# A GpSimd power over an unread 128x2 tile behind each of 512 transfers by index

## The chip, the core and the metric

The kernel runs on one core of a Trainium2 chip. A core has TensorE (PE in the profile, its weight loads PEld), VectorE (DVE), ScalarE (ACT), GpSimd (POOL) and SyncE (SP), each with an instruction stream of its own, run in the order written; they meet only at semaphores. Sixteen DMA engines move data for all of them. A DMA whose rows are picked by a table of indices is issued from GpSimd here, a DMA with transposition from SyncE. The metric is the time of one execution on the device in microseconds, the median of several.

## What is computed

A small transformer of two layers over x, 32 x 256 tokens of width 128, each step a residual:

```python
x = x + 0.5 * _L0_ffn_ref(_layernorm(x), ...)   # 8 experts, the best 2 of each token, and a shared one
x = x + _L0_attn_ref(_layernorm(x), ...)        # attention without softmax, group norm, projection
x = x + 0.5 * _L0_ffn_ref(_layernorm(x), ...)   # the same expert layer again
x = x + 0.5 * _L1_ffn_ref(x, ...)               # 8 experts, the best 1, gelu
x = x + _L1_attn_ref(x, ...)                    # gated linear attention, a scan over time
x = x + 0.5 * _L1_ffn_ref(x, ...)
```

The expert layer of the first kind is what the change touches. For each token it multiplies with the weights of two experts only:

```python
idx = jax.lax.top_k(biased, TOP_K)[1]
cw = jnp.sum(jax.nn.one_hot(idx, E) * weights[..., None], axis=1)
a = swiglu(h1 * h3)
routed = jnp.einsum('te,etd->td', cw, y)
```

## The kernel before

The 8192 tokens are 64 tiles of 128, in 16 chunks of four tiles; x stays on the chip. The tokens are dealt to the experts in three groups of 4, 6 and 6 chunks, and this happens in two passes (`l` is 0 and 1), one for each use of the expert layer. For a group:

- `head` normalizes a chunk and computes the logits of the router; `routed` (VectorE) picks the two experts of each token and writes for each tile the two places in memory that its rows go to (`r_slot`).
- `scatter`, on GpSimd, writes the 128 rows of a tile to memory at those places, once for each of the two picks: two DMAs by index a tile, so 32, 48 and 48 for a group (L1914). They count up `scattered[g]`.
- SyncE fills the ends of the experts' regions (`clear_ends`, L1965), waits for all of the group's scatters and then loads units of 512 sorted rows with transposed DMAs, four a unit (`load_rows`, L1979, into `u_xp`). TensorE multiplies a unit with the weights of its experts (L759), the results go to memory (`ys`). A group has 10, 14 and 14 units.
- `fetches`, on GpSimd, gathers the results back, eight DMAs by index a chunk (L1930, into `y_in`), and counts up `fetched`; VectorE adds them to x with their weights (`weighed`, L1135).

GpSimd also computes all reciprocal roots of the norms, as a power with the table `half_neg` (-0.5): the roots of the first layer norm (`rstd_entry`, L1880), those of the later heads (`rstd_head`, L1885, and the group norm's `gn_r_head` of 128x2, L1895), and the roots of the three later stages (L1874 and L1876). VectorE and ScalarE wait for these.

There is no scheduler at run time. A string of letters for each engine (`turns`) is an order written out by hand: "s" is a tile's two scatters, "f" one fetch, the other letters are steps of the heads, units and stages. So on GpSimd a root stands behind the transfers that the string puts before it, even where its input has long been there, and a transfer behind a root whose input is late.

Of the kernel before, what the change touches and what calls it, by code (L numbers as in the profile page):

```python
# [3 lines left out]

# [1 line left out]

# [8 lines left out]
ALU = mybir.AluOpType  # L15
# [3 lines left out]
P = 128  # L19
# [4 lines left out]
NB = T // BATCH_TILES  # L24
# [116 lines left out]
def build(nc, dram, packed, x_in, out):  # L141
# [14 lines left out]
    with ExitStack() as ctx:  # L156
# [48 lines left out]
        a1_wqkv, a1_wg = a1_w[:, 0:3 * D], a1_w[:, 3 * D:]  # L205
        half_neg = sb("half_neg", [P, T])
        limit_at = sb("limit_at", [P, 1])
        first_half = sb("first_half", [P, P])
        minus_sign = sb("minus_sign", [P, 1])
        of_parity = sb("of_parity", [P, 2])  # L210
# [22 lines left out]
        y_stored = [sem(f"y_stored{i}") for i in range(2)]  # L233
        fetched = [sem(f"y_fetched{i}") for i in range(2)]
        rows_in = [sem(f"rows_in{i}") for i in range(XP_BUFFERS)]
        n_loads = 7

        x = sb("x", [P, chunks * T, D])
# [1630 lines left out]
        def pool_program(pool):  # L1869
            on = Waiting(pool)  # L1870

            def root(s, which, c, a, b):
                on.wait_ge(*s.by_vector.at("mv", which, c))
                s.by_pool.mark(pool.tensor_scalar(s.ve[:], s.mv[:, :, 1], a, b, ALU.mult, ALU.add), "ve", which, c)  # L1874
                on.wait_ge(*s.by_pool.at("ve", which, c))
                s.by_pool.mark(pool.tensor_tensor(s.rstd[:], s.ve[:], half_neg[:], ALU.pow), "rstd", which, c)  # L1876

            def early(c):
                on.wait_ge(*entry.by_vector.at("ve", c))
                entry.by_pool.mark(pool.tensor_tensor(entry.rstd[:, c, :], entry.ve[:, c, :], half_neg[:], ALU.pow),  # L1880
                                   "rstd", c)

            def head_root(s, which, c):
                on.wait_ge(*s.by_vector.at("ve", which, c))
                s.by_pool.mark(pool.tensor_tensor(s.rstd[:], s.ve[:], half_neg[:], ALU.pow), "rstd", which, c)  # L1885

            def head(s, l, c, k):
                j = k - 11 if l else k
                if l and j == 0:
                    head_root(s, ("ffn0", l), c)  # L1890
                elif l and k == 1:
                    head_root(s, "attn0", c)
                elif l and k == 8:
                    on.wait_ge(*s.by_vector.at("gn_ve", c))
                    s.by_pool.mark(pool.tensor_tensor(s.gn["r"][:], s.gn["ve"][:], half_neg[:, 0:NB], ALU.pow),  # L1895
                                   "gn_r", c)

            def ffn1(s, c, k):
                if k == 1:
                    root(s, "ffn1", c, (1.0 + EPS) * X_SCALE ** -2, EPS * EPS * X_SCALE ** -2)  # L1900

            def attn1_front(c, k):
                if k == 0:
                    root(front, "attn1", c, 1.0 + RMS_EPS, EPS * RMS_EPS)

            def scatter(l, g, t):
                c = groups[g].first + t // T
                on.wait_ge(*route.by_vector.at("slot", l, c // 2))
                on.wait_ge(*heads[c % LANES].by_vector.at("rows", l, c))
                if l:  # L1910
                    for u in (groups[g].units - 2, groups[g].units - 1):
                        on.wait_ge(*unit_lanes[u % 2].by_tensor.at("h", l - 1, g, u, 0, 0))
                for i in range(2):
                    pool.indirect_dma_start(  # L1914
                        row_dram[g], bass.IndirectOffsetOnAxis(route.slot[g][:, i, t:t + 1].bitcast(U32), 0),
                        rows[:, groups[g].first * T + t, :, :].rearrange("p k d -> p (k d)"), None).then_inc(scattered[g], 16)

            def fetches(l, c, n):
                g, t0, i = group_of[c], (c - groups[group_of[c]].first) * T, c % 2
                k, t = divmod(n, T)  # L1920
                if n == 0:
                    for j in range(2):
                        last = load_index((l, g, groups[g].units - 1))
                        on.wait_ge(y_stored[(last + j) % 2], 16 * ((last + 1 + j) // 2))
                    on.wait_ge(*route.by_vector.at("result", l, g))
                    if l or c >= 2:
                        l2, c2 = divmod(l * chunks + c - 2, chunks)
                        reader = mids[c2 % 2] if l2 else heads[c2 % LANES]
                        on.wait_ge(*reader.by_vector.at("weighed", l2, c2, 1))
                pool.indirect_dma_start(  # L1930
                    fetch.y[i][:, t, k, :], None, y_dram[g],
                    bass.IndirectOffsetOnAxis(route.result[g][:, k, t0 + t:t0 + t + 1].bitcast(U32), 0)).then_inc(fetched[i], 16)

            visits = {"early": early, "head": head, "ffn1": ffn1, "front": attn1_front, "scatter": scatter,
                      "fetch": fetches}
            for name, what in order("pool"):
                if name in visits:
                    visits[name](*what)
# [250 lines left out]
```

## Time and profile before

| | |
|---|---|
| time, median of 3 runs | 1219.88 us (1218.39 to 1219.9) |
| the profiled execution: its own span, first to last instruction | 1611.3 us |
| granted TensorE clock, mean of that execution | 0.851 of full speed |
| GpSimd busy there | 645.2 us (40%), 679 instructions |
| VectorE, ScalarE, TensorE busy there | 1037.9, 881.7, 1208.2 us |

The profiled execution is 391 us longer than the median of the runs; no more is known of its time than its span. Busy is the time within instructions; an engine that waits for a semaphore, or for its next instruction, is idle. In the tables a row "<- issue" is idle time in which the engine waited for nothing that the profile shows.

### The profile page before, as it was taken

Reading aid. Unit: us, or ns where it says so; the run is one execution under the profiler, and the core shown is the slowest. Engines: PE = TensorE matmul, PEld = TensorE weight load, DVE = VectorE, ACT = ScalarE, POOL = GpSimd, SP = SyncE. Lnnn points to the kernel's source line nnn. Section 1 sums busy time; section 2 is a strip of 40 time slices with the busy share of each in tenths; the row PEclk is TensorE's granted clock in tenths of the full one; section 3 lists DMA queues with packets and bytes.
Section 4 is the critical chain, followed back from the end, with each engine's and each line's share of the span. In section 5 each row is a group of like instructions: output and inputs, shape, how many; then the busy total and the mean of one; then the engine's idle time right before and its main releaser. Section 6 shows DMA issues by size and latency. Waiting matters only on the chain.

```text
span 1611.3 us, 37336 instructions
## 1 busy us (share of the span) xinstructions
PE 1208.2 (75%) x14084; PEld 950.7 (59%) x14113; DVE 1037.9 (64%) x3441; ACT 881.7 (55%) x1505; POOL 645.2 (40%) x679
## 2 busy tenths in 40 slices
PE   3745767567766778767666766799989897989997
PEld 2423545455555666555554645677877676768776
DVE  7954655455645656666664664677767757888774
ACT  3545556334544445645543653676677445766764
POOL 1364443344555455555545453431322323342100
PEclk9876878787887978988887887898898978999989
DMA  8012323223132322222132222311210101010001
GB/s 263 14 50 62 79 68 75 59 63 83 57 84 70 78 71 76 62 65 55 57 87 67 68 67 66 76 43 46 56 46 23 28 18 33 15 29 24 2 9 34
DMA packets 172875, 93.77 MB, mean 58 GB/s; under 512 B 98516, under 2 KB 163183, under 8 KB 172575
## 3 DMA queue, kind: packets, MB, share of 16 engines
q1 hardware_dynamic: 115886, 35.64, 9.0%
q0 software_dynamic: 16384, 33.59, 7.3%
q10 hardware_dynamic: 40432, 22.17, 4.9%
q8 instruction: 118, 1.93, 0.5%
q14 instruction: 55, 0.44, 0.1%
HBM read 25.78 MB, written 45.61 MB: 44 GB/s over the span
## 4 chain that ended last, share of the span: by engine, by line
PE 37%; DVE 22%; ACT 13%; another core or an unknown queue 13%; issue 12%; POOL 1%; DMA 1%; ACTq 0%; POOLq 0%; DVEq 0%; SPq 0%
PE bank L759 8%; PE bank L581 3%; PE bank L820 2%; PE bank L967 2%; PE bank L806 2%; PE bank L839 2%; DVE x L1135 2%; PE bank L775 2%; PE sums L984 1%; PE sums L901 1%; PE bank L532 1%; PE sums L904 1%; ACT heads_store L1674 1%; DVE heads_store L1189 1%
## 5 line engine op out<-in xcount | busy, mean ns | idle before, releaser
L1914 POOL DMA_INDIRECT rows<-store,r_slot x256 | 258.8, 1011 | 185.1 <-DVE r_slot L1396 114.1
L759 PE MATMUL bank<-u_xp,w_hi 128*128 128x128 f16 x2432 | 267.3, 237 | 83.7 <-issue 74.0
L1930 POOL DMA_INDIRECT y_in<-ys,r_result x256 | 262.2, 1024 | 120.6 <-issue 70.3
L759 PE MATMUL bank<-u_xp,w_lo 128*128 128x128 f16 x1216 | 245.7, 237 | 34.6 <-issue 34.4
L759 PEld LDWEIGHTS bank<-u_xp,w_hi 128*128 x2432 | 212.3, 108 | 100.0 <-issue 94.4
L759 PEld LDWEIGHTS bank<-u_xp,w_lo 128*128 x1216 | 130.3, 107 | 47.1 <-issue 47.1
L581 PE MATMUL bank<-heads_store,w_hi 128*128 128x512 f16 x256 | 92.6, 449 | 7.0 <-DVE r_lg L1164 4.2
L1874 POOL TENSOR_SCALAR ve_last<-mv_last 128x4 f32<-128x4 f32 x16 | 3.1, 195 | 215.0 <-DVE mv_last L1092 214.9
L1698 ACT ACTIVATE heads_store<-bank,sc 128x512 f32<-128x512 f32 x64 | 43.3, 682 | 75.0 <-PE bank L581 41.1
L1135 DVE SCALAR_TENSOR_TENSOR x<-y_in,r_weight,x 128x128 f32<-128x128 f32 x256 | 72.5, 346 | 1.1
L1189 DVE TENSOR_TENSOR heads_store<-bank,heads_store 128x512 f32<-128x512 f32 x64 | 43.7, 686 | 42.7 <-ACT heads_store L1698 33.9
L1885 POOL TENSOR_TENSOR rstd_head<-ve_head,half_neg 128x4 f32<-128x4 f32 x32 | 34.6, 1082 | 88.1 <-DVE ve_head L1097 86.8
L1481 DVE TENSOR_TENSOR u_gated_even<-bank,u_gated_even 128x512 f32<-128x512 f32 x38 | 26.0, 685 | 66.7 <-ACT u_gated_even L1769 34.6
L1665 ACT COPY heads_store<-bank 128x1024 f16<-128x1024 f16 x32 | 32.3, 1009 | 54.6 <-remote 32.3
L967 PE MATMUL bank<-store 32*64 32x64 f32 x2048 | 49.6, 239 | 15.6 <-issue 12.1
L1625 DVE TENSOR_TENSOR store<-store,bank 128x512 f32<-128x512 f32 x64 | 40.9, 681 | 25.0 <-PE bank L967 14.9
L581 PE MATMUL bank<-heads_store,w_lo 128*128 128x512 f16 x128 | 56.7, 443 | 0.0
L1895 POOL TENSOR_TENSOR gn_r_head<-gn_ve_head,half_neg 128x2 f32<-128x2 f32 x16 | 11.9, 742 | 109.7 <-DVE gn_ve_head L1334 109.7
L967 PEld LDWEIGHTS bank<-store 32*64 32x64 f32 x2048 | 41.8, 149 | 22.8 <-issue 17.9
L1769 ACT ACTIVATE u_linear_odd<-bank,sc 128x512 f32<-128x512 f32 x38 | 26.0, 683 | 50.1 <-PE bank L759 25.9
L1481 DVE TENSOR_TENSOR u_linear_odd<-bank,u_linear_odd 128x512 f32<-128x512 f32 x38 | 26.1, 687 | 40.3 <-remote 15.7
L1769 ACT ACTIVATE u_gated_odd<-bank,sc 128x512 f32<-128x512 f32 x38 | 26.0, 684 | 47.1 <-remote 37.3
(434 smaller groups left out, 3478.4 us busy)
## 6 DMA issues: line engine op xcount, KB each, us to landing
ys<-u_y_even ACTq DMA_DIRECT2D x38, 256.0 KB
ys<-u_y_odd ACTq DMA_DIRECT2D x38, 256.0 KB
u_xp<-rows SPq DMA_TRANSPOSE x304
x<-x_dram SPq DMA_DIRECT2D x16, 256.0 KB, 5.6
rows<-store,r_slot POOLq DMA_INDIRECT x256
y_in<-ys,r_result POOLq DMA_INDIRECT x256
out_dram<-x SPq DMA_DIRECT2D x16, 256.0 KB
rows<-blank SPq DMA_DIRECT2D x48, 64.0 KB
```

The costliest lines, as they stand in the source:

```text
L581: ins = pe.matmul(B[:], wp[:, part, E, which, :], s.xp[:, xp, :], start=(n == 0), stop=(n == 2))
L759: ins = pe.matmul(B[:, of_block[j]], of_expert(wp, e, F16, part, which), xp_rows[:, xp, of_block[j]], start=(n == 0 and j == 0), stop=(n = ...
L967: ins = pe.matmul(B[i][halves[u], col:col + HALF], kt[strip[i], tokens], qpt[slot][strip[i], tokens], start=True, stop=True)
L1135: ins = dve.scalar_tensor_tensor(xt, y[:, t, i, :], w[:, i, t0 + t:t0 + t + 1], xt, ALU.mult, ALU.add)
L1189: s.by_vector.mark(dve.tensor_tensor(h, ring[s.name, "h", l, c, part, 1][:], h, ALU.mult), "h", l, c, part)
L1481: s.by_vector.mark(dve.tensor_tensor(h[:], ring["units", "h", l, g, u, part, 1][:], h[:], ALU.mult), "h", *use, part)
L1625: mark(dve.tensor_tensor(s.att[g], s.att[g], ring[s.name, "att", c, g][:], ALU.mult), "att", c, g)
L1698: s.by_scalar.mark(act.activation(t, ring[s.name, "h", l, c, part, 0][:], ACT.Copy, scale=sc31[:]), "h", l, c, part)
L1769: s.by_scalar.mark(act.activation(t[:], ring["units", "h", l, g, u, part, 0][:], ACT.Copy, scale=sc31[:]), "h", *use, part)
L1885: s.by_pool.mark(pool.tensor_tensor(s.rstd[:], s.ve[:], half_neg[:], ALU.pow), "rstd", which, c)
L1914: pool.indirect_dma_start(row_dram[g], bass.IndirectOffsetOnAxis(route.slot[g][:, i, t:t + 1].bitcast(U32), 0), rows[:, groups[g].first * ...
L1930: pool.indirect_dma_start(fetch.y[i][:, t, k, :], None, y_dram[g], bass.IndirectOffsetOnAxis(route.result[g][:, k, t0 + t:t0 + t + 1].bitc ...
```

## The change

GpSimd gets one more step behind each of its 512 DMAs by index: it raises two columns of a table of ones, [128, 2], to the power -0.5 and writes the result to a new tile `pace`, which nobody reads. Each such step waits for the semaphore that the one before it counted up, and counts it up itself. No other engine's program changes, and no other engine waits for `pace`.

```diff
+        pace = sb("pace", [P, NB])
...
+        pace_taken = sem("pace_taken")
...
         def pool_program(pool):
             on = Waiting(pool)
 
+            steps_taken = count(1)
+
+            def paced():
+                n = next(steps_taken)
+                if n > 1:
+                    on.wait_ge(pace_taken, n - 1)
+                pool.tensor_tensor(pace[:], const["ones"][:, 0:NB], half_neg[:, 0:NB], ALU.pow).then_inc(pace_taken, 1)
+
...
                     pool.indirect_dma_start(
                         row_dram[g], bass.IndirectOffsetOnAxis(route.slot[g][:, i, t:t + 1].bitcast(U32), 0),
                         rows[:, groups[g].first * T + t, :, :].rearrange("p k d -> p (k d)"), None).then_inc(scattered[g], 16)
+                    paced()
...
                 pool.indirect_dma_start(
                     fetch.y[i][:, t, k, :], None, y_dram[g],
                     bass.IndirectOffsetOnAxis(route.result[g][:, k, t0 + t:t0 + t + 1].bitcast(U32), 0)).then_inc(fetched[i], 16)
+                paced()
```

The first place is GpSimd's stream at the first scatters of the first group, in the first pass. Before (L1914 is a scatter, `rstd_entry` a root of the first layer norm; x2 is a run of two):

```order
L1880 TENSOR_TENSOR rstd_entry<-ve_entry,half_neg 128x4 x4
L1914 DMA rows<-store,r_slot 26624x256 x2
L1880 TENSOR_TENSOR rstd_entry<-ve_entry,half_neg 128x4
L1914 DMA rows<-store,r_slot 26624x256 x2
L1880 TENSOR_TENSOR rstd_entry<-ve_entry,half_neg 128x4 x2
```

Of the change, the same place (lines have moved: the scatter is L1924, the root L1890, the new step L1880; `w_packed` holds the table of ones):

```order
L1890 TENSOR_TENSOR rstd_entry<-ve_entry,half_neg 128x4 x4
L1924 DMA rows<-store,r_slot 26624x256
L1880 TENSOR_TENSOR pace<-w_packed,half_neg 128x2
L1924 DMA rows<-store,r_slot 26624x256
L1880 TENSOR_TENSOR pace<-w_packed,half_neg 128x2
L1890 TENSOR_TENSOR rstd_entry<-ve_entry,half_neg 128x4
L1924 DMA rows<-store,r_slot 26624x256
L1880 TENSOR_TENSOR pace<-w_packed,half_neg 128x2
L1924 DMA rows<-store,r_slot 26624x256
L1880 TENSOR_TENSOR pace<-w_packed,half_neg 128x2
```

Nothing has moved against anything else; a new step stands behind each DMA, also where a root or another DMA follows at once.

The second place is GpSimd's stream where scatters, fetches and roots are mixed (a fetch is L1930 before and L1941 in the change; `gn_r_head` is the root of the group norm). Before:

```order
L1930 DMA y_in<-ys,r_result 128x128 x3
L1895 TENSOR_TENSOR gn_r_head<-gn_ve_head,half_neg 128x2
L1930 DMA y_in<-ys,r_result 128x128
L1885 TENSOR_TENSOR rstd_head<-ve_head,half_neg 128x4
L1914 DMA rows<-store,r_slot 28672x256 x2
```

Of the change:

```order
L1941 DMA y_in<-ys,r_result 128x128
L1880 TENSOR_TENSOR pace<-w_packed,half_neg 128x2
L1905 TENSOR_TENSOR gn_r_head<-gn_ve_head,half_neg 128x2
L1941 DMA y_in<-ys,r_result 128x128
L1880 TENSOR_TENSOR pace<-w_packed,half_neg 128x2
L1895 TENSOR_TENSOR rstd_head<-ve_head,half_neg 128x4
L1924 DMA rows<-store,r_slot 28672x256
L1880 TENSOR_TENSOR pace<-w_packed,half_neg 128x2
L1924 DMA rows<-store,r_slot 28672x256
L1880 TENSOR_TENSOR pace<-w_packed,half_neg 128x2
```

Again the order of the old steps is kept, and each root and each transfer now stands behind one new step more for every transfer ahead of it. On the other four engines the order of instructions is the same before and after.

## Rows read from the trace of the kernel before

**Rows 1.** The page: busy time by engine; the chain that ended last, by engine.
```profile
PE 1208.2 (75%) x14084; PEld 950.7 (59%) x14113; DVE 1037.9 (64%) x3441; ACT 881.7 (55%) x1505; POOL 645.2 (40%) x679
...
PE 37%; DVE 22%; ACT 13%; another core or an unknown queue 13%; issue 12%; POOL 1%; DMA 1%; ACTq 0%; POOLq 0%; DVEq 0%; SPq 0%
```

**Rows 2.** Stretches of the span; each engine's busy us (instructions), clock, DMA share, GB/s.
```profile
0.00:58.50 58.50, 30.46 (x185) 21.33 (x185) 47.15 (x184) 24.89 (x41) 4.60 (x11) 1.00 0.60 181
58.50:275.00 216.50, 138.91 (x1221) 93.67 (x1222) 131.54 (x444) 118.45 (x195) 102.82 (x102) 0.75 0.23 63
275.00:618.50 343.50, 236.06 (x2190) 188.78 (x2188) 186.21 (x622) 158.81 (x259) 168.16 (x169) 0.82 0.27 70
618.50:981.00 362.50, 249.17 (x2230) 193.53 (x2229) 218.40 (x783) 182.61 (x300) 200.12 (x201) 0.85 0.27 69
981.00:1457.60 476.60, 415.49 (x5771) 341.05 (x5791) 347.57 (x1086) 299.95 (x533) 156.25 (x175) 0.87 0.15 38
1457.60:1611.30 153.70, 138.07 (x2498) 112.37 (x2505) 106.99 (x325) 96.98 (x180) 13.29 (x22) 0.95 0.06 16
```

**Rows 3.** Waits of POOL from 58.5 to 981 us: total us, times, longest.
```profile
POOL rows L1914 <- DVE r_slot L1396: 114.1, 11, 22.3
POOL gn_r_head L1895 <- DVE gn_ve_head L1334: 109.7, 15, 14.0
POOL rstd_head L1885 <- DVE ve_head L1097: 86.8, 19, 10.5
POOL rows L1914 <- issue: 70.8, 241, 0.3
POOL y_in L1930 <- issue: 42.7, 148, 0.3
```

**Rows 4.** Waits of POOL from 981 to 1457.6 us.
```profile
POOL y_in L1930 <- issue: 27.9, 100, 0.3
```

**Rows 5.** Waits of PE over the span, then from 58.5 to 981 us.
```profile
PE bank L759 <- issue: 108.4, 122, 3.8
...
PE bank L759 <- issue: 102.3, 116, 3.8
```

**Rows 6.** Timelines of POOL and of PE in the same unit: start, us, what, idle before.
```profile
818.08 0.94 POOL L1930 DMA_INDIRECT y_in<-ys,r_result  x1 [0.30 <-issue]
819.33 0.95 POOL L1930 DMA_INDIRECT y_in<-ys,r_result  x1 [0.30 <-issue]
...
823.42 0.26 PE L759 MATMUL bank<-u_xp,w_hi 128*128 128x128 f16 x1 [1.32 <-issue]
824.86 0.26 PE L759 MATMUL bank<-u_xp,w_hi 128*128 128x128 f16 x1 [1.17 <-issue]
```

**Rows 7.** POOL's timeline: two DMAs, a 128x2 power, two DMAs.
```profile
760.04 0.96 POOL L1914 DMA_INDIRECT rows<-store,r_slot  x1 [0.30 <-issue]
761.31 0.96 POOL L1914 DMA_INDIRECT rows<-store,r_slot  x1 [0.30 <-issue]
762.28 0.73 POOL L1895 TENSOR_TENSOR gn_r_head<-gn_ve_head,half_neg 128x2 f32<-128x2 f32 x1
763.21 1.02 POOL L1930 DMA_INDIRECT y_in<-ys,r_result  x1 [0.20 <-issue]
764.54 1.08 POOL L1930 DMA_INDIRECT y_in<-ys,r_result  x1 [0.30 <-issue]
```

**Rows 8.** POOL's groups: line, operation, tiles, count, busy us, mean ns.
```profile
L1895 POOL TENSOR_TENSOR gn_r_head<-gn_ve_head,half_neg 128x2 f32<-128x2 f32 x16 | 11.9, 742 | 109.7 <-DVE gn_ve_head L1334 109.7
```

**Rows 9.** Busy time of L1914 alone, then of L1930 alone, by stretch.
```profile
58.50:275.00 216.50, 90.06 (x90) 0.75 0.23 63
275.00:618.50 343.50, 70.68 (x70) 0.82 0.27 70
618.50:981.00 362.50, 98.05 (x96) 0.85 0.27 69
...
275.00:618.50 343.50, 77.45 (x78) 0.82 0.27 70
618.50:981.00 362.50, 73.00 (x74) 0.85 0.27 69
981.00:1457.60 476.60, 111.71 (x105) 0.87 0.15 38
```

**Rows 10.** Timeline: group 1's last scatter and first transposed load; another group's load, its unit.
```profile
119.28 0.96 POOL L1914 DMA_INDIRECT rows<-store,r_slot  x1 [0.30 <-issue]
122.99 1.29 SPq L1979 DMA_TRANSPOSE u_xp<-rows  x1
...
806.42 22.14 SPq L1979 DMA_TRANSPOSE u_xp<-rows  x16
...
815.25 0.28 PE L759 MATMUL bank<-u_xp,w_hi 128*128 128x128 f16 x2
```

**Rows 11.** Tile y_in: L1135's durations in ns (min/median/max), first and last start.
```profile
L1135 DVE SCALAR_TENSOR_TENSOR x<-y_in,r_weight,x x256: 252/347/380, 317.3 to 1468.8; 128x128 f32<-128x128 f32 x128
```

More of the change, by code:

```diff
@@ L2 @@
 from contextlib import ExitStack
-from itertools import repeat
+from itertools import count, repeat
 import numpy as np
```

## The prediction

> **What bounds the kernel now.** I read the busy times first [rows 1]. No engine is full: TensorE is busy 75% of the profiled span, VectorE 64%, GpSimd 40%. By that view GpSimd, which alone gets more work, could take a lot. But the profiled execution spans 1611.3 us and the median of the runs is 1219.9, so 391 us of what the trace shows, most of it idle time, is not there when it counts. The instructions themselves can't have been slowed by a third: VectorE's 1038 busy us would be 85% of 1220. So I ask next where the extra idle time sits.
>
> TensorE shows it in the product of the units, L759: 108.4 us idle before its matmuls with no cause, 102.3 of them between 58.5 and 981 us [rows 5]. In one unit it issues one matmul every 1.44 us (823.42, 824.86) where nothing is waited for. On GpSimd nothing like it is seen: in the same unit its transfers start every 1.25 us (818.08, 819.33) with 0.30 us of issue between them [rows 6], as they do elsewhere [rows 7], and 0.3 is the longest issue gap of its transfers [rows 3, 4]. I conclude that the execution without a profile is shorter in the waiting of the other engines, above all ahead of 981 us, and that GpSimd's stream costs about the same in it.
>
> So I count how much of the time GpSimd's stream fills. From 58.5 us (its first scatter) to 981 us (its last; 922.5 us) it is busy 102.8 + 168.2 + 200.1 = 471.1 us [rows 2], and the issue gaps between transfers are 70.8 + 42.7 = 113.5 us [rows 3]: 584.6 us occupied, 337.9 idle. From 981 to 1457.6 us, its last fetch, 156.3 + 27.9 = 184.2 us are occupied, 292.4 idle [rows 2, 4]. Ahead of and behind these, 58.5 and 153.7 us hold no transfer.
>
> **The change part by part.** *The new step.* The nearest row is the group norm's root, the same operation of the same shape: 742 ns in the mean of 16 [rows 8]. Its price in the stream is less, since it covers an issue gap: with it between them two transfers start 1.90 us apart (761.31 to 763.21) and without it 1.27 (760.04 to 761.31), and the transfer behind it takes 1.02 instead of 0.96 us [rows 7]. With a step behind every transfer I expect a cycle of 1.02 + 0.01 + 0.73 + 0.20 = 1.96 us, 0.70 above 1.27. The bounds are 0.63 (1.90 - 1.27) and 0.74. The Trainium skill's page "Perfetto Trace Analysis", section "GPSIMD Engine Instruction", says the same of the method: a GpSimd span is not to be trusted, the start-to-start spacing is. By the span the 512 steps would come to 380 us, by the spacing to 358. The trace bears the rule out, with a span of 0.73 that costs 0.63 to 0.70.
>
> *The wait.* Each step waits for the one before it, which had a whole transfer of 0.96 us to finish [rows 7]. I price it at nothing; at worst it is an issue gap of 0.2 us, since a root with a wait, such as the one of rows 7, starts 0.01 us behind its transfer.
>
> *Where it falls.* From 58.5 to 981 us stand 90 + 70 + 96 = 256 scatters and 78 + 74 = 152 fetches [rows 9]: 408 x 0.70 = 286 us. Behind 981 us stand 104 fetches (105 with one cut at the edge): 73 us. The last new step comes behind the last fetch, so the final stretch gains nothing.
>
> *Who waits for it.* Behind each new step stand the next transfer and the next root. The last scatter of a group releases SyncE's transposed loads: the first group's is issued at 119.28 and the first load at 122.99; another group's loads begin at 806.42 and TensorE takes its first unit at 815.25 [rows 10]. A group's last batch is 16 scatters, so 11 us later at each. A root delayed by n transfers is n x 0.70 us later for VectorE and ScalarE, and through the order written out for all that stands behind.
>
> *The sum.* In the profiled span both stretches have idle time above the added work (338 against 286, 292 against 73), so there the growth should be modest: I expect 1611 to become 1690 to 1780 us, since a stream in fixed order cannot use all its idle time. Without the profile the idle time is smaller. If the 391 us are spread evenly, each stretch lasts 1219.9 / 1611.3 = 0.757 of its length. The first is then 698 us, of which 585 are occupied and 114 idle; 286 - 114 = 172 us stay over, and the end comes at 1392 us. The second is 361 us with 177 idle, against 73: hidden, at most 20 us lost in waits between. If the 391 us sit mostly ahead of 981 us, as rows 5 suggest, the first stretch has no idle time left (it can't be shorter than its 585 us), all 286 us show, and the end comes at 1506 us. Against that the 0.30 us gaps may themselves be partly the profile's; were they gone altogether, 113 us more could be absorbed, 286 - 114 - 113 = 59 us stay, 1279 us. I take 1410, a little above the even split, because rows 5 weigh more than the doubt on the gaps, and idle time between fixed waits is never used up whole.
>
> **The rivals.** *The idle time absorbs most of it (1240 to 1340 us).* If GpSimd's instructions shrink with everything else, the profile's own balance holds: 338 idle against 286. Then only what is exposed at the groups' ends counts, 6 x 11 = 67 us, times 0.757 = 51: 1271 us. For it: GpSimd is 1% of the chain that ended last [rows 1], and 311 of its 338 idle us are waits for VectorE (114.1, 109.7 and 86.8 us) [rows 3]. Against it: 0.96 us per transfer does not vary where TensorE's issue stalls.
>
> *It is hidden altogether (1220 us).* That needs every transfer to be waited for by nobody. Rows 10 speak against it: loads follow the last scatter within 4 us. That the change does not do what it says belongs here, but all 512 steps stand in the compiled order.
>
> *Faster (about 1200 us).* The transfers, spaced at 1.96 instead of 1.27 us, could leave room on the DMA engines for the transposed loads and for whatever holds TensorE to one matmul in 1.44 us [rows 6]. It decides for a gain only once the stalls that it removes outweigh what stays over of 286 us; all of L759's stalls are 108.4 us [rows 5], times 0.757 = 82, and a quarter of these, 20 us, would do only if everything else were hidden. The DMA engines' mean share is 0.23 to 0.27 there [rows 2], so there is little crowding to relieve.
>
> *More than all of it (above 1480 us).* The full price of both stretches is 1220 + 359 = 1579 us. It needs no idle time absorbed in either. A lower TensorE clock would help it: in the stretch of 0.75 granted clock TensorE is also the least busy, 139 of 216.5 us [rows 2], and a slower stream makes it idle more.
>
> *VectorE is held off.* The Trainium skill's page "SBUF — State Buffer", section "Who interferes with whom", says that a GpSimd instruction that reads SBUF and a VectorE instruction with two SBUF inputs exclude each other, the second waiting until the first ends. L1135 has two such inputs, and its 256 instructions take 347 ns in the median and 380 at most [rows 11], so the trace shows no such wait at any of them, though few of them can have met one of the rare powers of the kernel before. By the rule each of the 256 could wait up to one step, 0.73 us, 187 us in all; by the row at most 0.03 us each, 8 us. It is in the case above 1480 with little weight.
>
> **How the numbers follow.** GpSimd's stream as the new bound, 1360 to 1480 us: 0.60. Mostly absorbed, 1240 to 1360: 0.20. Above 1480: 0.12. Hidden (within 0.2%, about what a measurement of this kernel tells from no change): 0.04. Faster: 0.04. The range 1285 to 1490 leaves out about two in ten: hidden and faster, the lower part of the second case, and most of the case above. Faster 0.04, same 0.04, slower 0.92.
>
> **What would show it.** In the profile of the changed kernel: 512 instances of the new line at 0.72 to 0.75 us; transfers 1.96 us apart in a run (wrong below 1.8 or above 2.1: the price); GpSimd busy 645 + 380 = 1025 us; the first load of the first group some 11 us later than 122.99; waits of VectorE and ScalarE for GpSimd's roots that now are counted in tens of us. A span that grows by under 40 us together with a time that grows by over 100 would confirm that the idle time of the profile is its own. The prediction is wrong if GpSimd's instructions turn out shorter without a profile (then 1271), or if the time that it waits for VectorE is a chain that it doesn't lengthen. It is wrong on the other side if idle time can't be used at all.

## The result and the profile after

The changed kernel takes 1506.51 us (median of 4 runs, 1502.78 to 1510.26) against 1219.86 us (4 runs, 1218.39 to 1219.9) for the kernel before: ratio 1.2346, 95% interval 1.2306 to 1.2386, 286.6 us slower. The direction and the engine that becomes the bound are as forecast. The time is 97 us above the forecast of 1410 and 17 above the range.

The kernel before itself has two levels, about 1220 us and about 1600 us, each held by all its runs of a comparison, while the changed kernel takes 1503 to 1520 us beside either. The profile that the prediction was read from (span 1611.3 us) is one of the upper level. The profile of the change spans 1504.3 us in an execution of 1506.29 us. No trace of the kernel before at the lower level exists.

The page of the changed kernel, busy time and the chain that ended last by engine and by line:

```profile
PE 1124.2 (75%) x14084; PEld 912.0 (61%) x14113; DVE 1038.1 (69%) x3441; ACT 877.6 (58%) x1505; POOL 1067.9 (71%) x1191
...
POOL 56%; DVE 16%; PE 14%; issue 8%; ACT 5%; DMA 1%; POOLq 0%; SPq 0%; DVEq 0%; ACTq 0%
POOL pace L1880 22%; POOL rows L1924 18%; POOL y_in L1941 12%; POOL rstd_head L1895 2%; PE bank L822 2%; DVE x L1137 1%; PE bank L841 1%; PE bank L969 1%; PE bank L761 1%; DVE store L1627 1%; POOL rstd_entry L1890 1%; PE sums L986 1%; PE ba
```

Against [rows 1] GpSimd goes from 1% of the chain to 56%, and 22% of it is the new line alone. VectorE's busy time has not moved (1038.1 against 1037.9). Three groups of the changed kernel: line, operation, tiles, count, then busy us and mean ns, then idle time ahead:

```profile
L1880 POOL TENSOR_TENSOR pace<-w_packed,half_neg 128x2 f32<-128x2 f32 x512 | 398.9, 779 | 16.1
L1924 POOL DMA_INDIRECT rows<-store,r_slot x256 | 277.2, 1083 | 69.5 <-issue 46.2
...
L1941 POOL DMA_INDIRECT y_in<-ys,r_result x256 | 273.8, 1070 | 50.9 <-issue 45.3
```

GpSimd's timeline in the changed kernel at the end of the first group's scatters, then SyncE's first transposed load:

```profile
128.61 1.03 POOL L1924 DMA_INDIRECT rows<-store,r_slot  x1 [0.19 <-issue]
129.68 0.72 POOL L1880 TENSOR_TENSOR pace<-w_packed,half_neg 128x2 f32<-128x2 f32 x1
130.60 1.03 POOL L1924 DMA_INDIRECT rows<-store,r_slot  x1 [0.20 <-issue]
...
133.00 1.28 SPq L1991 DMA_TRANSPOSE u_xp<-rows  x1
```

The cycle, from the start of one transfer to the start of the next, is 1.99 us here, close to the 1.96 worked out beforehand from [rows 7]; over all 430 pairs of transfers with nothing but a new step between them its median is 1.988 and its mean 2.075 us. In the kernel before 421 pairs of transfers that follow each other at once have 1.276 and 1.322. The first load comes 10.0 us later than in [rows 10]. But against this upper-level trace later ones come earlier: the fifth group's load starts at 771.6 us against 806.4.

Five waits of the changed kernel, longest totals first (engine, line, what it waits for, total us, times, longest):

```profile
POOL ve_last L1884 <- DVE mv_last L1094: 155.9, 12, 27.5
...
DVE gn_sc_head L1340 <- POOL gn_r_head L1905: 61.7, 16, 9.2
...
DVE heads_store L1105 <- POOL rstd_head L1895: 58.8, 13, 12.3
PE bank L761 <- DMA u_xp<-rows: 55.9, 8, 28.3
...
DVE away_head L1155 <- POOL rstd_head L1895: 48.5, 15, 6.1
```

and of TensorE for its own issue, which was 108.4 us in [rows 5]:

```profile
PE bank L761 <- issue: 1.5, 2, 1.1
```

GpSimd waits once more for VectorE, ahead of its first scatter; from there to its last scatter, 885 us later, none of its waits is longer than 0.2 us. In the kernel before three rows of such waits come to 311 us [rows 3], of which 22 stand ahead of the first scatter too. The first scatter and the last:

```profile
58.36 1.46 POOL L1924 DMA_INDIRECT rows<-store,r_slot  x1 [22.29 <-DVE r_slot L1398]
...
942.26 1.03 POOL L1924 DMA_INDIRECT rows<-store,r_slot  x1 [0.20 <-issue]
```

So two things happened. VectorE now waits for GpSimd's roots, as forecast, and TensorE for loaded rows. And against the trace of before, the matmuls that were issued at one in 1.44 us [rows 6] are gone: the stall that the rival "faster" named is relieved. Relief against an upper-level profile and price together make 1504 of 1611. That at the lower level there is nothing to relieve, so that the price alone shows, fits the 287 us but is argued: no trace shows the kernel before there.

### The profile page after: what moved, and what is told of

It reads as the page before. It is cut to its first block, busy times and chain, and to the rows that moved or that the text cites. A ratio compares the mean times of both kernels' runs of the same rounds, so it can differ in the third digit from the quotient of the medians.

```text
span 1504.3 us, 37848 instructions
## 1 busy us (share of the span) xinstructions
PE 1124.2 (75%) x14084; PEld 912.0 (61%) x14113; DVE 1038.1 (69%) x3441; ACT 877.6 (58%) x1505; POOL 1067.9 (71%) x1191
## 4 chain that ended last, share of the span: by engine, by line
POOL 56%; DVE 16%; PE 14%; issue 8%; ACT 5%; DMA 1%; POOLq 0%; SPq 0%; DVEq 0%; ACTq 0%
POOL pace L1880 22%; POOL rows L1924 18%; POOL y_in L1941 12%; POOL rstd_head L1895 2%; PE bank L822 2%; DVE x L1137 1%; PE bank L841 1%; PE bank L969 1%; PE bank L761 1%; DVE store L1627 1%; POOL rstd_entry L1890 1%; PE sums L986 1%; PE bank L808 1%; PE bank L885 1%; POOL gn_r_head L1905 1%
## 5 line engine op out<-in xcount | busy, mean ns | idle before, releaser
L1880 POOL TENSOR_TENSOR pace<-w_packed,half_neg 128x2 f32<-128x2 f32 x512 | 398.9, 779 | 16.1
L1924 POOL DMA_INDIRECT rows<-store,r_slot x256 | 277.2, 1083 | 69.5 <-issue 46.2
L761 PE MATMUL bank<-u_xp,w_hi 128*128 128x128 f16 x2432 | 240.9, 231 | 97.5 <-DMA u_xp<-rows 55.9
L1941 POOL DMA_INDIRECT y_in<-ys,r_result x256 | 273.8, 1070 | 50.9 <-issue 45.3
L1137 DVE SCALAR_TENSOR_TENSOR x<-y_in,r_weight,x 128x128 f32<-128x128 f32 x256 | 73.0, 346 | 27.6 <-DMA y_in<-ys,r_result 26.4
L841 PE MATMUL bank<-a_w,heads_store 128*128 128x408 f32 x128 | 53.0, 557 | 17.3 <-ACT heads_store L1664 17.0
L774 PE MATMUL bank<-by_expert,r_member 128*128 128x128 bf16 x304 | 33.2, 239 | 40.1 <-DVE u_linear_odd L1476 16.2
L1771 ACT ACTIVATE u_gated_even<-bank,sc 128x512 f32<-128x512 f32 x38 | 25.9, 682 | 63.1 <-PE bank L761 61.0
L534 PE MATMUL bank<-w_packed,heads_store 128*128 128x128 f32 x128 | 25.0, 328 | 49.6 <-DVE heads_store L1105 44.3
L1664 ACT COPY heads_store<-bank 128x512 f32<-128x512 f32 x32 | 18.7, 583 | 71.5 <-PE bank L534 36.6
L1105 DVE TENSOR_SCALAR heads_store<-x,mv_head,rstd_head 128x128 f32<-128x128 f32 x64 | 19.6, 372 | 58.8 <-POOL rstd_head L1895 58.8
L774 PEld LDWEIGHTS bank<-by_expert,r_member 128*128 128x128 bf16 x304 | 23.0, 107 | 48.5 <-issue 14.2
```

Of the source, the lines that this page charges most:

```text
L534: ins = pe.transpose(M[:, by_t[t]], s.xn[:, t, :], ident[:])
L761: ins = pe.matmul(B[:, of_block[j]], of_expert(wp, e, F16, part, which), xp_rows[:, xp, of_block[j]], start=(n == 0 and j == 0), stop=(n = ...
L774: pe.matmul(Y[:, of_block[j]], members(use)[:, j:j + 1].broadcast_to([P, BLOCK]), by_expert[:, 0, :], start=(j == 0), stop=False, skip_gro ...
L841: s.by_tensor.mark(pe.matmul(B[:, 0:3 * D + 3 * NH1], s.xt[:, by_t[t]], a1_w[:], start=True, stop=True), "qkv", c, t)
L1137: ins = dve.scalar_tensor_tensor(xt, y[:, t, i, :], w[:, i, t0 + t:t0 + t + 1], xt, ALU.mult, ALU.add)
L1880: pool.tensor_tensor(pace[:], const["ones"][:, 0:NB], half_neg[:, 0:NB], ALU.pow).then_inc(pace_taken, 1)
```

## The experiments

Unless the diff says otherwise, edits are to the changed kernel. "Beside" means the kernel before, run in turn with it. In the comparison of the result the kernel before was at the lower level. Of the five that follow, four met the upper level (runs 1 to 4, 5 to 8, 9 to 12 and 16 to 18) and one the lower (13 to 15).

**1. The kernel before, once more.** No edit.

> The kernel before, unchanged, profiled once more. My theory takes the 391 us that its profiled execution was longer than its timed ones for that one execution's own (TensorE issuing one matmul in 1.4 us beside the transposed loads), so a second profile should span either about 1218 us or again far more than the timed runs. At about 1218 us the GpSimd stream up to its last scatter should be nearly without idle time (under 100 us). Rival, that GpSimd has ample idle time and the growth comes from elsewhere: over 200 us of idle time there.

1608.8 us, beside 1605.3; ratio 1.0026 (0.9993 to 1.0059). The profile is like that of [rows 1]: GpSimd is busy 645.7 us in a span of 1600.3 (645.2 in 1611.3), and TensorE's issue stalls in the product of the units are 94.1 us (108.4). Of the two forecasts the rival's holds, ample idle time on GpSimd, but at the upper level only. Each of these runs has a span about 2 us below its time, so the difference of 391 us is not time outside the span.

**2. A step behind the scatters only.**

```diff
                     bass.IndirectOffsetOnAxis(route.result[g]...)).then_inc(fetched[i], 16)
-                paced()
```

> A step behind each of the 256 scatters only, none behind the fetches. If GpSimd's stream bounds the kernel up to the last scatter from the start, each of the 256 steps counts in full at 0.7 to 0.8 us: 1395 to 1425 us. If the stream first had about 120 us of idle time to fill and only what is over it shows (406 us of price against 287 of growth), 200 us of steps give 1290 to 1320 us. If VectorE is held off by reads of GpSimd, half the steps give half the growth: 1363 us.

1509.6 us, beside 1605.3; ratio 0.941 (0.9366 to 0.9454). That this is the time of the full change with half its steps is a coincidence of two parts: the last scatter ends at 901.6 us against 943.3, and what stands behind it lasts 603 us against 561.

**3. A step behind the fetches only.**

```diff
                         rows[:, ...].rearrange("p k d -> p (k d)"), None).then_inc(scattered[g], 16)
-                    paced()
```

> A step behind each of the 256 fetches only; about 152 of these stand ahead of the last scatter in the trace of before. Bound from the start: 152 x 0.75 = 114 us and little behind it: 1330 to 1350 us. Idle time filled first: 1220 to 1270 us. VectorE held off: 1363 us, as in the run with scatters only.

1486.8 us; ratio 0.9267 (0.9237 to 0.9298).

**4. A step behind the second pass's fetches only.**

```diff
                     bass.IndirectOffsetOnAxis(route.result[g]...)).then_inc(fetched[i], 16)
-                paced()
+                if l:
+                    paced()
```

and none behind the scatters.

> A step behind the 128 fetches of the second pass only, most of which stand behind the last scatter. If a step costs nothing where GpSimd waits for VectorE: 1220 to 1245 us. If each step costs by itself, through VectorE or the DMA queue: a quarter of the growth, 1290 us.

1561.1 us; ratio 0.9731 (0.9673 to 0.9789). Behind the last scatter, where most of its steps stand, it lasts 591 us against 629 in run 1; between the first scatter and the last it is 906 against 913. In all three the steps made the kernel faster than the one beside it, and none of the forecasts of runs 2 to 4, which were all written for a kernel before of 1220 us, can be read against the result. That was the surprise of the study, and led to the next run.

**5. The change again, beside the kernel before at the upper level.** No edit.

> The changed kernel, unchanged. In the last runs the kernel before took 1605 us, as in its profiled execution, and not 1220 as in the three timed ones; so the 391 us are no artefact of one execution. Theory A: the transfers issued back to back hold up the other engines' issue (TensorE at one instruction per 1.4 us), and a step between them relieves that, so the change takes about 1506 us again, and where the kernel before takes 1605 it is the faster one, ratio 0.94. Theory B: the long state is the chip's, and the change adds its 287 us to it: 1890 us, ratio 1.18.

1509.9 us, beside 1609.4: ratio 0.9419 (0.9365 to 0.9472). The change's time is that of the first comparison within 0.3%; what differs is the kernel before. Theory A's 1506 us holds; theory B, that the upper level is a state of the chip to which the change adds its 287 us, fell here.

**6. A short step in place of the power.**

```diff
-                pool.tensor_tensor(pace[:], const["ones"][:, 0:NB], half_neg[:, 0:NB], ALU.pow).then_inc(pace_taken, 1)
+                pool.memset(pace[:], 1.0).then_inc(pace_taken, 1)
```

> The power is replaced with a memset of the same 128x2 tile, with the same wait and count; such a step took about 0.1 us at the start of the trace. If it is the time between transfers that relieves the others (Theory A by spacing), 0.1 us relieves little: 1560 to 1605 us. If any instruction of another kind between two transfers does, the relief comes without the price: 1220 to 1400 us. Theory B: 1605 + 512 x 0.1 = 1656 us.

1606.2 us, beside 1609.4; ratio 1.0002 (0.9958 to 1.0046), a microsecond above the forecast's 1560 to 1605. Its timeline on GpSimd:

```profile
62.42 1.06 POOL L1924 DMA_INDIRECT rows<-store,r_slot  x1
63.48 0.27 POOL L1880 MEMSET pace<- 128x2 f32 x1
63.78 0.98 POOL L1924 DMA_INDIRECT rows<-store,r_slot  x1
```

512 more instructions with 512 more waits cost nothing: the transfers start 1.36 us apart at this place and 1.321 in the mean, as without the clears (1.322), so the clears lie in the issue gap that stood there anyway. TensorE's issue stalls stay (107.0 us). Neither the wait nor the instruction is what costs or relieves; the length is.

**7, 8, 9. A step behind every second, every fourth, every third transfer.**

```diff
+            behind = count(1)
+
             def paced():
+                if next(behind) % 2:
+                    return
```

(4 and 3 in the other two).

> The power behind every second transfer only, 256 in all. The runs with scatters only and with fetches only, also 256, took 1510 and 1487 us. Theory A: price and relief both halve from 1605: 1470 to 1520 us. Theory B: 1605 + 143 = 1748 us.

> The power behind every fourth transfer only, 128 in all. Theory A: between the kernel before and the half dose, 1530 to 1570 us, as the run with 128 steps in the second pass (1561). If a rare break were enough for the relief, below 1470 us. Theory B: 1605 + 72 = 1677 us.

> A step behind every third transfer (170). Relief against price: between the kernels of every fourth (1460 us) and of every second (1400 us), at 1420 to 1445 us, with 5 to 15 stalls of TensorE. If only a gap behind every second transfer removes them, it is at or above 1460 us.

1400.2 us for every second, beside 1609.4: ratio 0.8726 (0.8628 to 0.8824); 1460.4 for every fourth: 0.9101 (0.9036 to 0.9167); 1413.9 for every third, beside 1616.4: 0.874 (0.863 to 0.885). TensorE's waits for its own issue in the product of the units, every second, every fourth, every third:

```profile
PE bank L761 <- issue: 19.8, 48, 1.2
```

```profile
PE bank L761 <- issue: 74.8, 124, 2.1
```

```profile
PE bank L761 <- issue: 41.7, 78, 4.3
```

Each is one kernel's row of the same wait. Both theory A's forecasts (1470 to 1520 and 1530 to 1570 us) and that for every third (1420 to 1445) lay too high: the relief grows faster than the dose. As the steps grow from 0 to 128, 170, 256 and 512 this wait falls from 108 to 75, 42, 20 and 2 us; the time falls from 1605 to 1460, 1414 and 1400, and is back at 1510 with 512. From 256 steps on there is hardly a stall left to remove, and what is added only lengthens GpSimd's stream (32% of the chain with 256 steps, 56% with 512).

The row of L759 is only a part of what is relieved. The chain of the kernel before holds "another core or an unknown queue", 13% of 1611 us [rows 1], where the profile names nothing that ended a wait. Its piece in the unit of [rows 6], from that kernel's chain and timeline:

```profile
818.46 10.96 another core or an unknown queue
...
829.44 0.69 ACT L1769 ACTIVATE u_gated_even<-bank,sc 128x512 f32<-128x512 f32 x1 [10.98 <-remote]
```

By the program this step of ScalarE waits for TensorE's matmuls alone, the unit's product L759 among them, and the 11 us are the stretch in which these matmuls were issued at one in some 1.4 us. So at this place the unknown queue is the same stall, seen from ScalarE. The row is 13, 14 and 15% of the chain in three profiles of the kernel before, 12% with the clears, 8, 6 and 2% with a step behind every fourth, third and second transfer, and absent in the changed kernel.

**10. 256 steps, two at a time behind every fourth transfer.**

```diff
+                if next(behind) % 4:
+                    return
+                for _ in range(2):
+                    n = next(steps_taken)
+                    ...
```

> 256 steps as in the kernel with a step behind every second transfer (1400 us), but two at a time behind every fourth one: GpSimd's stream gets the same work, and four transfers still follow each other without a gap, as in the kernel with one step behind every fourth (1460 us). If runs of transfers without a gap are what holds up TensorE's issue, its stalls stay as in the kernel of every fourth (some 20 of 0.9 to 2 us in the product of the units, 75 us of issue idle time) and the time is 1460 to 1540 us. If it is the mean rate of the transfers that counts, the stalls are gone as with every second and the time is about 1400 us.

1423.9 us, beside 1616.4; ratio 0.8802 (0.874 to 0.8865); issue stalls 29.0 us, and 13 single issue gaps of 0.9 to 2 us in these matmuls, against 24 with one step behind every fourth. Neither forecast was met cleanly: most of the relief comes with the mean rate of the transfers, and 24 us of it are lacking beside the steps spread evenly (1400.2). It is not the runs of transfers without a gap by themselves.

**11. Two steps behind each transfer.**

```diff
+                for _ in range(2):
                     n = next(steps_taken)
                     if n > 1:
                         on.wait_ge(pace_taken, n - 1)
                     pool.tensor_tensor(...)
```

> Two powers in place of one behind each transfer by index (1024 steps). The second waits for the first, so it should cost its full 0.73 us or a little more in the stream. If GpSimd's stream is the bound once one step stands behind each transfer, each of the 408 steps ahead of the last unit group's end shows in full: 408 x 0.75 = 306 us and up to 78 us in the final stretch, so 1815 to 1890 us. The rival, that the 289 us in which GpSimd is still idle in the changed kernel take up a good part of it, gives 1600 to 1720 us.

1875.4 us, beside 1616.4: 368 us above the changed kernel's 1507, or 0.72 us for each of the 512 further steps, and in the forecast's first range. Of this kernel, the page's first row and chain by engine:

```profile
PE 1169.5 (63%) x14084; PEld 948.2 (51%) x14113; DVE 1039.7 (56%) x3441; ACT 880.4 (47%) x1505; POOL 1444.2 (77%) x1703
...
POOL 67%; DVE 11%; PE 9%; issue 8%; ACT 4%; DMA 1%; POOLq 0%; SPq 0%; DVEq 0%; ACTq 0%
```

The cycle is 2.887 us in the mean, 0.812 above the change's; times 408 that is 331 us for the part up to the last scatter (its end moves by 322, from 943.3 to 1265.4 us), and 37 are left for the rest. The rival with 1600 to 1720 us is out: with one step behind each transfer the stream has no give left ahead of the last scatter.

**12. The kernel before, its fetches as ordinary transfers.**

```diff
-                pool.indirect_dma_start(
-                    fetch.y[i][:, t, k, :], None, y_dram[g],
-                    bass.IndirectOffsetOnAxis(route.result[g][:, k, t0 + t:t0 + t + 1].bitcast(U32), 0)).then_inc(fetched[i], 16)
+                pool.dma_start(fetch.y[i][:, t, k, :], y_dram[g][(t0 + t) * P:(t0 + t + 1) * P, :]).then_inc(fetched[i], 16)
```

> The kernel before, without any added step; the 256 fetches of results take fixed rows with an ordinary transfer from GpSimd's queue in place of rows by index, so the sums that follow use other rows. The 256 scatters by index stay. If runs of transfers by index hold up the issue of the other engines, the stalls of TensorE fall at least by half and the time falls by 100 to 250 us from 1605 us. If any transfer does it, or if it is not the transfers at all, the time stays within 40 us of 1605 us.

1368.5 us, beside 1616.4; ratio 0.8459 (0.8412 to 0.8507). Its wait:

```profile
PE bank L759 <- issue: 54.0, 63, 2.5
```

Half the transfers by index are gone, and so is half of 108.4 us; the time fell by 248 us. GpSimd's stream is shorter too (0.57 us a transfer), but GpSimd is 1% of the chain before and here, so its shorter stream alone hardly makes 248 us. Both parts of the first forecast hold, the halving of the stalls only just.

**13, 14, 15. No transfer by index at all; then with one, then with two steps behind each.** Run 13 is the kernel before with this edit, 14 and 15 are the changed kernel with it. Scatters go to fixed rows of a buffer of their own and the loads read fixed blocks of it; fetches are as in 12.

```diff
-                    pool.indirect_dma_start(
-                        row_dram[g], bass.IndirectOffsetOnAxis(route.slot[g][:, i, t:t + 1].bitcast(U32), 0),
-                        rows[:, ...].rearrange("p k d -> p (k d)"), None).then_inc(scattered[g], 16)
+                    at = (i * groups[g].tiles + t) * P
+                    pool.dma_start(
+                        aside[g][at:at + P, :],
+                        rows[:, ...].rearrange("p k d -> p (k d)")).then_inc(scattered[g], 16)
...
-                                           block_rows(row_dram[g], firsts[j])).then_inc(...)
+                                           block_rows(aside[g], (PER_UNIT * u + j) % (groups[g].picks // BLOCK) * BLOCK)).then_inc(...)
```

> The kernel before with no transfer by index at all: the 256 scatters go with ordinary transfers from GpSimd's queue to fixed rows of a buffer of their own, from which the transposed loads then read fixed blocks, and the 256 fetches take fixed rows. The numbers computed differ, the amount of data and all waits stay. With the fetches alone replaced the time was 1368 us. If the transfers by index are what separates 1605 from the 1220 us of the first comparison, it is 1200 to 1280 us and TensorE's stalls in the product of the units (34 us of issue idle time with the fetches replaced) are gone. If the level comes from elsewhere, it stays at 1340 to 1380 us.

> The same, with one power behind each of the 512 ordinary transfers. An ordinary transfer took 0.57 us of GpSimd in the kernel with plain fetches, so a cycle is about 0.57 + 0.01 + 0.73 + 0.02 to 0.2 = 1.35 to 1.5 us, close to the 1.27 us of the kernel before. If it is the length of GpSimd's stream that costs, below a bound of its own the steps are hidden and the time stays within 30 us of the kernel without steps. If each step costs wherever it stands, it is 200 to 290 us above it.

> The same with two powers behind each ordinary transfer: a cycle of about 2.1 us, as in the changed kernel (2.08), with no transfer by index in it. If the changed kernel's 1507 us are set by the length of GpSimd's stream alone, this kernel takes about as long, 1480 to 1560 us. If the transfers by index themselves are part of what its time is made of, it takes under 1440 us.

(The 34 us in the first of these is a slip: run 12's row has 54.0.) Here the kernel before took 1221.7 us (15 runs, 1216 to 1232, spans 1214.2 to 1230.2, granted clock 0.957 to 0.976): the lower level, and with spans, so it is no matter of whether an execution is recorded. Without a step 1209.6 us, ratio 0.9894 (0.9847 to 0.9941); with one 1220.8, 0.9984 (0.9944 to 1.0023); with two 1547.9, 1.2691 (1.2566 to 1.2815). The cycles are 0.547, 1.350 and 2.180 us in the mean (the kernel before: 1.322, the change: 2.075). First rows and chains, with one step and with two:

```profile
PE 1063.7 (87%) x14113; PEld 855.4 (70%) x14113; DVE 1027.1 (84%) x3441; ACT 875.4 (72%) x1505; POOL 803.5 (66%) x1191
...
DVE 31%; POOL 27%; PE 22%; ACT 13%; issue 4%; DMA 2%; SPq 0%; ACTq 0%; POOLq 0%; DVEq 0%
```

```profile
PE 1144.1 (74%) x14113; PEld 928.6 (60%) x14113; DVE 1031.4 (67%) x3441; ACT 878.1 (57%) x1505; POOL 1177.9 (76%) x1703
...
POOL 62%; DVE 15%; PE 14%; issue 4%; ACT 4%; DMA 1%; POOLq 0%; SPq 0%; DVEq 0%
```

This is the cleanest answer on the change, and all three times are in their forecast ranges. The same 512 steps behind transfers that leave room for them cost 11 us. Brought to the cycle of the changed kernel and 0.105 us more, with no transfer by index, the kernel takes 41 us more than the changed one; 408 x 0.105 = 43. What sets the changed kernel's time is the length of GpSimd's stream and nothing particular to transfers by index. What run 13 can't settle is its own question: the kernel beside it was already at 1222 us with its transfers by index, so 1209.6 us doesn't show that these transfers make the upper level.

**16, 17, 18. The kernel before, the change, and every second step together.** No new edits.

> The kernel before, unchanged, for a profile beside the two that follow. Three chips gave it 1605 to 1616 us and one gave 1222 us (15 runs with spans of 1214 to 1230 us), so the level goes with the chip and not with the recording. On a chip of the lower level I expect a span of about 1220 us, GpSimd's transfers by index 1.27 us apart as elsewhere, the granted clock at 0.97, and no stalls of TensorE in the product of the units (L759 after issue under 20 us against 108 us); on one of the upper level 1605 us again.

> The change, unchanged. Its time is set by the length of GpSimd's stream, so it should be 1500 to 1515 us at either level of the kernel before. If it were made of the same stalls as the upper level of the kernel before, it would be lower on a chip of the lower level, under 1450 us.

> A step behind every second transfer. On a chip of the upper level 1400 us again, faster than the kernel before. On a chip of the lower level there is nothing to relieve, and the line through the runs in which GpSimd's stream is the bound gives 1507 - 256 x 0.72 = 1323 us for it (1300 to 1345), which is slower than the kernel before by 8%; if the relief were of another kind and also worked there, it would stay at or below 1222 us.

1583.1, 1517.6 and 1392.1 us, beside 1589.9: ratios 0.9937 (0.9882 to 0.9992; the same kernel, so about what the upper level's own spread leaves), 0.9553 (0.9388 to 0.9719) and 0.8763 (0.8612 to 0.8913). The change lies 3 us above its forecast of 1500 to 1515. It was the upper level again, on the chip that had given the lower one in runs 13 to 15. So the first sentence of the expectation of run 16, that the level goes with the chip, is false. The issue wait of TensorE was back:

```profile
PE bank L759 <- issue: 107.8, 113, 6.9
```

## Why the prediction was right in kind and wrong in size

*Price of a step: nearly right.* 0.70 us a step was read from one undisturbed place [rows 7], and where nothing else happens the spacing is 1.99 us as worked out (1.96). Over a whole stream it is 2.075 against 1.322, 0.753 us: in the mean a power takes 779 ns, not 730, and a transfer 1076, not 1020, while the cycle before is 1.32, not 1.27. That adds 0.053 x 512 = 27 us to the full price of 359.

*The wait: right.* Run 6 has all of the waits, and costs nothing.

*Idle time absorbed ahead of the last scatter: the term that failed.* With the profile's idle time shrunk evenly, by 0.757, I took 114 of 286 us as absorbed in the first stretch and let 172 stay over. Measured, the price of the same 408 steps is 408 x 0.753 = 307 us, of which 287 show: 20 us are absorbed, not 114. In the changed kernel GpSimd has no wait left between its first scatter and its last, as shown above. The 104 steps behind it (78 us) are hidden, as I had them. So the term is off by 94 us; with 21 for the price that is 115, less the 18 by which my 1410 stood above the even split's 1392: the miss of 97. (I read the last scatter at 981 us; it ends at 977.7, with three fetches less ahead of it, which is 2 us of price.) Run 11 shows the same from the other side, where each further step costs 0.72 us.

*The even split was the wrong picture.* The sum with "no idle time left" ahead of 981 us gives 1506, the measured time to the us, and I gave it less weight. That the numbers agree to the us is luck: the price that it takes is 21 us too low and the idle time 20. The picture is borne out by where the last scatter stands, read in each trace:

| kernel | span, us | end of the last scatter | from there to the end |
|---|---|---|---|
| before, upper level | 1611.3 | 977.7 | 633.5 |
| change | 1504.3 | 943.3 | 561.0 |
| run 13, no transfer by index | 1207.4 | 650.3 | 557.1 |
| run 14, with one step | 1223.5 | 678.4 | 545.1 |
| run 15, with two | 1548.8 | 981.3 | 567.5 |

Where TensorE's issue stalls are gone, the part behind the last scatter lasts 545 to 568 us. If it does in the kernel before at 1220 us too, its last scatter ends at 650 to 673 us there, so that from the first scatter, at 58 us, 592 to 615 us pass, of which 585 are occupied and 7 to 30 idle. That is an estimate, since no profile of that level exists. Of the 391 us some 305 to 328 would then lie ahead of the last scatter, where the even split has 224. Run 14 agrees: at 1220.8 us and a cycle of 1.350 us GpSimd is already 27% of the chain. From there 408 steps' worth of a longer cycle give 1221 + 408 x (2.075 - 1.350) = 1517 us, and 1507 was measured.

*"The idle time of the profile is its own": wrong.* I expected a span of 1690 to 1780 us with a time far below it. The span is 1504.3 us and the time 1506.29. The profile of before differed from the listed runs because it stood at another level of the kernel. For "GpSimd's stream costs about the same in it" there is a sign: the changed kernel's mean cycle is 2.075 us in the comparison at the lower level and 2.077 and 2.073 in runs 5 and 17 at the upper. For the kernel before itself it can't be read.

*The rival "faster": its mechanism was real, its cap too low.* I allowed it at most 82 us, all of L759's stalls, and a low share of DMA time spoke against it. At the upper level the relief is worth 209 us with 256 steps, price already paid (1609 to 1400), more than L759's own stalls; the unknown queue's share of the chain falls from 13 to 2% with it, some 206 to some 30 us, and at the place shown it is TensorE's stall. Where the kernel before takes 1220 us the change brought no gain. Run 18 was to say what every second step does at that level; it met the upper one, so this stays untried.

*Full price of both stretches (1579 us), hidden, mostly absorbed:* out. *VectorE held off:* the changed kernel's L1137, durations in ns (min/median/max), with 512 powers near it:

```profile
L1137 DVE SCALAR_TENSOR_TENSOR x<-y_in,r_weight,x x256: 253/346/397, 279.5 to 1361.9; 128x128 f32<-128x128 f32 x128
```

The median is that of [rows 11] (347) and the maximum grew by 17 ns, so none of the 256 waited for a power of 0.73 us to end. Of the 256, 69 start while a power is running, and these take 345 ns in the mean and 352 at most; the longer ones have no power beside them. With 1024 powers (run 11) the mean of all is 348 ns. This trace does not agree with the exclusion that the Trainium skill's page "SBUF — State Buffer", section "Who interferes with whom", states, as I read it: a GpSimd instruction that reads SBUF and a VectorE instruction with two SBUF inputs would wait for each other.

*What stays open.* Which of its two levels the kernel before takes. It is not the recording (run 13's comparison has spans at the lower level), not the chip (the same one gave both), and not the program (it is the same at both). At the upper level TensorE is issued at one instruction in 0.7 to 1.4 us while transfers by index follow each other, and spacing them, or replacing half of them, takes much or all of that away: that is shown. What in the chip holds the issue up no run here shows. Whether the lower level is the one in which exactly these stalls are missing is only argued; what speaks for it is that the changed kernel, which has none of them, takes the same time beside either level.

## What to carry to other kernels

Before idle time is subtracted from added work, ask whether the profiled execution is of the same level as the listed runs. A span a third above the listed time is first a sign of another level, not of idle time that can be scaled.

For an engine whose work runs in a written order, the length of its undisturbed cycle times the number of its transfers is a better guide than its share of busy time. GpSimd's 40% [rows 1] was of an upper-level span; up to its last scatter its stream alone fills 585 us, and one power behind each transfer made it the bound.

A filler instruction behind each transfer can help and hurt in one kernel: compare a dose of none, a quarter, a half and all before judging it. Here every second is the best of the upper level (1400 us, 13% faster than the kernel beside it), and of the versions that keep the whole computation only the change itself was measured beside the kernel before at 1220 us, 23% slower.

## What the runs showed of the hardware that was not expected

- While transfers by index ran back to back (1.27 us apart) at the upper level, TensorE in the same program was issued at one instruction in up to 1.44 us with nothing to wait for; 0.7 us of other GpSimd work behind every second one removed four fifths of that (108 to 20 us) and a clear of 0.13 us did nothing (107 us).
- An ordinary transfer of the same 128 rows holds GpSimd 0.55 to 0.59 us, one by index 1.01 to 1.08; the ordinary ones follow each other without the gap of 0.30 us.
- A power of 128x2 takes 0.72 us alone and two in a row 1.49 (run 15); a clear of the same tile has a span of 0.13 us in the mean and adds nothing to the spacing of the transfers (run 6).
- The mean granted clock was 0.975 in the execution that spans 1207.4 us, 0.888 in the one of 1504.3 and 0.806 in the one of 1870.3, and TensorE's busy time for the same work grew from 1060.2 to 1124.2 and 1169.5 us.
